# A streamed factorization-machine kernel: the last four input groups as two pairs of 32 KB rows instead of four single ones

## The chip, the core and the metric

The kernel runs on one core of one Trainium2 chip. The metric is the time of one execution in microseconds (us), as the median of several. A core has TensorE (PE in the profile; PEld is its weight load), VectorE (DVE), ScalarE (ACT), GpSimd (POOL) and SyncE (SP), each with its own instruction stream, and 16 DMA engines that move data between the main memory and the on-chip memory SBUF. Engines wait for each other by semaphores.

## The reference

```python
x_reg = input_data @ W_lin.T + b_lin                       # input_data: 1024 x 12500, f32
emb = input_data @ factors                                 # factors: 12500 x 16
sum_squared = jnp.square(emb.sum(axis=1))
squared_sum = (jnp.square(input_data) @ jnp.square(factors)).sum(axis=1)
h = jax.nn.relu(emb @ W1.T + b1)                           # 128
h = jax.nn.relu(h @ W2.T + b2)                             # 64
dnn_out = h @ W3.T + b3
x = x_reg + 0.5 * (sum_squared - squared_sum)[:, None] + dnn_out
x = 0.5 + jax.nn.sigmoid(x) * 5.0
```

The input is 51.2 MB and is read once. All else is small.

## The kernel before

The 12500 dimensions are cut into 97 chunks of 128, one dimension to a partition, and a rest of 84. The 1024 samples are columns. For each chunk TensorE multiplies the chunk of x by 17 weights (16 factors and the linear weight) and the squares of that chunk by 18 (only the last is not zero: minus half the sum of squared factors). Both add into a PSUM bank `p_lin`. VectorE and ScalarE make the squares (`squares`: 3 chunks by VectorE, 3 and 2 by ScalarE). GpSimd copies the weights of a group into small rings `wr` and `wz`.

The input comes in three parts, all issued by SyncE in one queue, in this order:

- 20 **groups** (g = 0 to 19, `TOTAL`) of 8 chunks by 512 samples, 2 MB each. Groups 0 to 11 are the first half of the samples, 12 to 19 two thirds of the second half. They land in six slots of the SBUF buffer `xr`, group g in slot g mod 6.
- The last 32 chunks of the second half, the **end**, in nine **pieces** (`PIECES`, index i): four of 352 samples (12, 10, 6 and 4 chunks; the middle block), then five of 160 samples (8, 8, 8, 6 and 2 chunks; the last block). They land in slots 2 to 5 of `xr` again.

Groups 0 to 15 (`PAIRED` = 16) come two to a transfer of 4 MB, with rows of 32 KB in each partition; groups 16 to 19 come one to a transfer of 2 MB with rows of 16 KB, and each has a semaphore of its own.

The order on TensorE is written out by hand. For a pair (`pair`, line 560) it is: wait for the landing, the matmuls on x of both groups (`multiply` twice), then those on the squares of both (`add_squares` twice). For a single group (lines 661 to 664): wait, `multiply`, `add_squares`. The last matmul of `add_squares` adds one to the semaphore `sq_used`, which starts at `RING` = 3. A slot of `xr` is free when `sq_used` says that its group is done, and SyncE waits for that before each transfer (lines 269, 273, 280):

- pair p waits for group 2p + 1 - 6, so the pair of groups 14 and 15 waits for group 9;
- single group g waits for group g - 6;
- the first two end pieces wait for group 17, the next two for group 18, the other five for group 19.

The end pieces are multiplied by `multiply_end` and `squares_end`, a block's small network (`layer1`, `layer2`, `layer3`, the embedding sums and squares) is woven between them, and SyncE stores each block's result.

Of the kernel before, what the change touches and what calls it, by code (L numbers as in the profile page):

```python
# [14 lines left out]
P = 128  # L15
# [4 lines left out]

REST = N % P
HALF = B // 2
CHUNKS = 8
TWO = 2
SLOTS = 6
RING = 3
ENDS = 32  # L30
ALL = (N - REST) // P
GROUPS = (ALL - 1) // CHUNKS
END_GROUPS = ENDS // CHUNKS
TOTAL = 2 * GROUPS - END_GROUPS
PAIRED = 16
W_END = ALL - ENDS

END_SLOT = TOTAL % SLOTS
# [11 lines left out]

PITCH = CHUNKS * HALF + 64
PAIR_PITCH = TWO * CHUNKS * HALF + 64

# [27 lines left out]
HD = HD_L + REST_SETS * LIN  # L84

def fm_kernel(nc, head, x_first, x_rest, x_pairs, x_groups, x_end, out):
    with ExitStack() as ctx:
        def sb(name, shape, dt=F32):
            return ctx.enter_context(nc.sbuf_tensor(name, shape, dt))  # L90
# [4 lines left out]
        def sem(name):  # L95
            return ctx.enter_context(nc.semaphore(name))
# [4 lines left out]
        xr = sb("xr", [P, SLOTS, CHUNKS, HALF])  # L101
# [33 lines left out]
        first_landed = sem("first_landed")  # L135
        rest_landed = sem("rest_landed")
        x_landed = [sem(f"x_landed{t}") for t in range(SLOTS // TWO)]
        single_landed = [sem(f"single_landed{g}") for g in range(PAIRED, TOTAL)]
        end_landed = [sem(f"end_landed{i}") for i in range(len(PIECES))]
        y_stored = sem("y_stored")  # L140
        zero_set = sem("zero_set")
# [91 lines left out]

            engine.wait_ge(x_landed[s // TWO], 16 * (r + 1))

        def single(engine, g):
            engine.wait_ge(single_landed[g - PAIRED], 16)

        def chunks(i):
            return sum(PIECES[i][2]) + sum(PIECES[i][3])  # L240

# [18 lines left out]
        @block.sync  # L260
        def _(sp):
            sp.dma_start(hd[:, :], head).then_inc(hd_landed, 16)  # L262
            sp.dma_start(xf[:, :], x_first).then_inc(first_landed, 16)  # L263
            sp.dma_start(xl[:, :, :].rearrange("p c b -> p (c b)"), x_rest).then_inc(rest_landed, 16)  # L264
            for p in range(PAIRED // TWO):
                at = TWO * p % SLOTS
                if TWO * p >= SLOTS:

                    sp.wait_ge(sq_used, RING + TWO * p + TWO - SLOTS)
                sp.dma_start(xr[:, at:at + TWO].rearrange("p s c b -> p (s c b)"),  # L270
                             x_pairs[p, :, 0:TWO * CHUNKS * HALF]).then_inc(x_landed[at // TWO], 16)
            for g in range(PAIRED, TOTAL):
                sp.wait_ge(sq_used, RING + g + 1 - SLOTS)
                sp.dma_start(xr[:, g % SLOTS].rearrange("p c b -> p (c b)"),
                             x_groups[g - PAIRED, :, 0:CHUNKS * HALF]).then_inc(single_landed[g - PAIRED], 16)
            at = 0
            for i in range(len(PIECES)):
                c, n = PIECES[i][1], chunks(i)
                rows = x_end[at:at + P * n * width(i)].rearrange("(p m) -> p m", p=P)
                sp.wait_ge(sq_used, RING + TOTAL - SLOTS + END_SLOT + last_slot(i) + 1)  # L280
                sp.dma_start(piece(i, c, n), rows).then_inc(end_landed[i], 16)
                at += P * n * width(i)

            for k in range(len(BLOCKS)):
                sp.wait_ge(y_ready[k], 1)
                sp.dma_start(out[cols(k)].rearrange("(q b) -> q b", q=4), y[0:P:32, line(k)]).then_inc(y_stored, 16)
            sp.wait_ge(y_stored, 16 * len(BLOCKS))
# [26 lines left out]
        @block.scalar  # L314
        def _(act):
            act.wait_ge(zero_set, 1)
            nc.scalar.activation(warm[:, :], zero[:, 0:1], ACT.Sigmoid)
            act.wait_ge(first_landed, 16)
            nc.scalar.activation(sqf[:, :], xf[:, :], ACT.Square).then_inc(first_squared, 1)  # L319

            def squares(r, s):

                act.wait_ge(sq_used, SLOTS * r + s + 1)
                c = BY_DVE
                for n in BY_ACT:
                    nc.scalar.activation(sq[:, ring(s), c:c + n, :], xr[:, s, c:c + n, :],  # L326
                                         ACT.Square).then_inc(act_squared, 1)
                    c += n

            def square_end(i, j=0):  # L330
                c = PIECES[i][1] + sum(PIECES[i][2][:j])
                n = PIECES[i][2][j]
                if j == 0:
                    act.wait_ge(end_landed[i], 16)
                    act.wait_ge(sq_used, squares_free(i))
                nc.scalar.activation(squared_piece(i, c, n), piece(i, c, n),  # L336
                                     ACT.Square).then_inc(act_end_squared, 1)

            def copy_lin(k, u):
                nc.scalar.copy(lin[:, part(k, u)], p_lin[k][:, u * BLOCKS[k][1] // 2:(u + 1) * BLOCKS[k][1] // 2]  # L340
                               ).then_inc(lin_ready[k], 1)

            def layer1(k, n):
                act.wait_ge(p_h1_done[k], 1)
                c = BLOCKS[k][0]
                nc.scalar.activation(h1[:, c:c + n], p_h1[0][:, 0:n], ACT.Relu,
                                     bias=pr[:, C_B1:C_B1 + 1]).then_inc(h1a_ready[k], 1)

            def embedding_square(k):
                act.wait_ge(p_es_done[k], 1)  # L350
                nc.scalar.activation(gsq[:, line(k)], tot_bank(k)[:, line(k)], ACT.Square).then_inc(gsq_ready[k], 1)

            def sigmoid(k):
                act.wait_ge(p_tot_done[k], 1)
                nc.scalar.activation(sg[:, line(k)], tot_bank(k)[:, line(k)], ACT.Sigmoid,
                                     bias=bias[:, :]).then_inc(sg_ready[k], 1)

            with act.Fori(0, GROUPS // SLOTS) as r:
                for s in range(SLOTS):
                    landed(act, r, s)  # L360
                    squares(r, s)

            act.wait_ge(sq_used, RING + GROUPS)
            copy_lin(0, 0)
            copy_lin(0, 1)
            layer1(0, BLOCKS[0][1] // 2)
            embedding_square(0)
            act.wait_ge(bias_ready, 1)
            sigmoid(0)

            for g in range(GROUPS, PAIRED):
                landed(act, g // SLOTS, g % SLOTS)
                squares(g // SLOTS, g % SLOTS)
            for g in range(PAIRED, TOTAL):
                single(act, g)
                squares(g // SLOTS, g % SLOTS)

            square_end(0, 0)
            square_end(0, 1)
            square_end(1, 0)  # L380
            square_end(1, 1)
            square_end(2)
            square_end(3)
            square_end(4, 0)
            act.wait_ge(p_lin_done[1], 1)
            copy_lin(1, 0)
            copy_lin(1, 1)
            nc.scalar.copy(rest[:, :], p_lin[1][:, BLOCKS[1][1]:HALF]).then_inc(rest_copied, 1)
            embedding_square(1)
            square_end(4, 1)  # L390
            layer1(1, BLOCKS[1][1])
            square_end(5, 0)
            square_end(5, 1)
            square_end(6, 0)
            square_end(6, 1)
            square_end(7, 0)
            square_end(7, 1)
            square_end(8)
            sigmoid(1)
            embedding_square(2)  # L400
            act.wait_ge(squares_done, 1)
            nc.scalar.copy(qs[:, :], p_sq[:, 0:BLOCKS[LAST][1]]).then_inc(qs_ready, 1)
            sigmoid(2)

        @block.vector
        def _(dve):
# [16 lines left out]
            def squares(r, s):  # L423

                dve.wait_ge(sq_used, SLOTS * r + s + 1)
                nc.vector.tensor_tensor(sq[:, ring(s), 0:BY_DVE, :], xr[:, s, 0:BY_DVE, :], xr[:, s, 0:BY_DVE, :],  # L426
                                        ALU.mult).then_inc(dve_squared, 1)
# [39 lines left out]
            layer2(0)  # L467
            scale(0)

            for g in range(GROUPS, PAIRED):  # L470
                landed(dve, g // SLOTS, g % SLOTS)
                squares(g // SLOTS, g % SLOTS)
            for g in range(PAIRED, TOTAL):
                single(dve, g)
                squares(g // SLOTS, g % SLOTS)

            square_end(0, 0)
# [24 lines left out]
        def _(pe):  # L502
# [40 lines left out]
            def multiply(r, s, h):  # L543
                pe.wait_ge(wr_ready, SLOTS * r + s + 1)
                for c in range(CHUNKS):
                    add_mm(quad(p_lin[h], c, LIN, 0, HALF), wr[:, ring(s), c, :], xr[:, s, c, :])
# [109 lines left out]
            embedding_square(0)  # L656
            layer3(0)

            for g in range(GROUPS, PAIRED, TWO):
                pair(g // SLOTS, g % SLOTS, 1)  # L660
            for g in range(PAIRED, TOTAL):
                single(pe, g)
                multiply(g // SLOTS, g % SLOTS, 1)
                add_squares(g // SLOTS, g % SLOTS, 1)

            pe.wait_ge(ws_ready, 2)
            for i in range(3):
# [102 lines left out]
```

## Time and profile before

| | us |
|---|---|
| median of 3 runs | 133.88 (133.85 to 133.91) |
| the profiled execution's own time | 133.95 |
| its span in the trace | 132.2 |

| engine | busy us | share of the span |
|---|---|---|
| TensorE, matmuls | 106.2 | 80% |
| TensorE, weight loads | 33.9 | 26% |
| ScalarE | 63.3 | 48% |
| VectorE | 52.5 | 40% |
| GpSimd | 15.5 | 12% |
| SyncE's DMA queue | 52.23 MB | 93.0% of 16 engines |

The span runs from the first to the last instruction in the trace; what lies around it is in the execution's own time. Matmuls are pipelined and their ends are modelled, so a row's time and its successor's start overlap a little: the start of the next row is the better measure of how long work took.

### The profile page before, as it was taken

What the parts mean: (1) busy time and instruction counts of PE and PEld (TensorE: products, weight loads), DVE (VectorE), ACT (ScalarE), POOL (GpSimd) and SP (SyncE); (2) the same over time, 40 slices, a digit from 0 to 9 for tenths busy, and PEclk for the clock granted to TensorE, in tenths of its full rate; (3) what the DMA queues carried; (4) which work ended last, traced back from release to release, by engine and by line L of the source; (5) the groups of instructions that cost most, each with busy time, mean ns of one, the idle gap of its engine ahead of it and who ended that gap; (6) DMA issues with size and microseconds to landing.
All of it is one profiled execution on the core that took longest, in us unless ns stands there. A gap on an engine that the chain in (4) does not pass through costs nothing.

```text
span 132.2 us, 2665 instructions
## 1 busy us (share of the span) xinstructions
PE 106.2 (80%) x1123; PEld 33.9 (26%) x1123; DVE 52.5 (40%) x51; ACT 63.3 (48%) x72; POOL 15.5 (12%) x48
## 2 busy tenths in 40 slices
PE   6089569939839739969649979999997975999992
PEld 4012112112112112212112233222221111335881
DVE  0391063037036036045055016565352351576571
ACT  4030067039139039049059046869562572465851
POOL 3015000110200200110200110064530000000000
PEclk9999968999999977999986999999999999999999
DMA  4999999999999999999999999999999999999700
GB/s 127 409 514 417 426 426 451 426 417 446 417 436 422 446 436 417 426 446 426 426 436 436 426 426 446 392 412 422 436 422 436 417 422 433 408 397 416 284 20 1
DMA packets 3489, 52.36 MB, mean 396 GB/s; under 512 B 404, under 2 KB 536, under 8 KB 1560
## 3 DMA queue, kind: packets, MB, share of 16 engines
q1 hardware_dynamic: 3480, 52.23, 93.0%
q8 instruction: 7, 0.11, 0.4%
q14 instruction: 2, 0.02, 0.0%
HBM read 52.22 MB, written 0.00 MB: 395 GB/s over the span
## 4 chain that ended last, share of the span: by engine, by line
DMA 54%; PE 39%; SPq 2%; DVE 1%; issue 1%; ACT 1%
DMA xr<-in_x_pairs 43%; PE p_lin L504 34%; DMA xr<-in_x_end 11%; PE p_h L600 2%; PE p_sq L504 2%; SPq L270 1%; PE p_tot L504 1%; PE p_h L631 1%; DVE h L452 0%; DVE h L447 0%; PE p_tot L613 0%; SPq L264 0%; SPq L263 0%; SPq L262 0%; ACT lin L340 0%
## 5 line engine op out<-in xcount | busy, mean ns | idle before, releaser
L326 ACT ACTIVATE sq<-xr 128x1536 f32<-128x1536 f32 (+1 forms) x40 | 47.7, 1260 | 45.1 <-DMA xr<-in_x_pairs 37.6
L426 DVE TENSOR_TENSOR sq<-xr 128x1536 f32<-128x1536 f32 x20 | 34.5, 1760 | 53.7 <-DMA xr<-in_x_pairs 42.9
L504 PE MATMUL p_lin<-xr,wr 128*17 128x512 f32 x320 | 41.4, 659 | 16.1 <-DMA xr<-in_x_pairs 14.2
L504 PE MATMUL p_lin<-sq,wz 128*18 128x512 f32 x320 | 36.6, 592 | 0.0
L504 PEld LDWEIGHTS p_lin<-xr,wr 128*17 128x17 f32 x320 | 9.3, 105 | 46.4 <-issue 39.6
L304 POOL COPY wr<-hd 128x136 f32 (+1 forms) x20 | 9.1, 454 | 75.2 <-PE p_lin L504 75.2
L504 PEld LDWEIGHTS p_lin<-sq,wz 128*18 128x18 f32 x320 | 9.5, 98 | 25.0 <-issue 23.7
L504 PE MATMUL p_lin<-xr,hd 128*17 128x352 f32 (+1 forms) x128 | 10.1, 380 | 1.8 <-DMA xr<-in_x_end 1.8
L435 DVE TENSOR_TENSOR sq<-xr 128x1408 f32<-128x1408 f32 (+3 forms) x6 | 6.6, 1133 | 6.2 <-DMA xr<-in_x_end 6.2
L336 ACT ACTIVATE sq<-xr 128x1408 f32<-128x1408 f32 (+3 forms) x6 | 5.7, 981 | 6.3 <-DMA xr<-in_x_end 6.3
L504 PE MATMUL p_lin<-sq,ws 128*18 128x352 f32 x64 | 6.7, 459 | 0.0
L504 PE MATMUL p_lin<-xf,hd 128*17 128x512 f32 x4 | 3.6, 1049 | 3.5 <-DMA xf<-in_x_first 3.5
L504 PEld LDWEIGHTS p_lin<-xr,hd 128*17 128x17 f32 x128 | 4.3, 97 | 5.9 <-issue 4.1
L305 POOL COPY wz<-s_all 128x8 f32 (+1 forms) x20 | 5.4, 271 | 0.0
L435 DVE TENSOR_TENSOR xr<-xr 128x320 f32<-128x320 f32 (+1 forms) x9 | 3.8, 450 | 2.1 <-DMA xr<-in_x_end 2.1
L504 PE MATMUL p_sq<-xr,ws 128*18 128x160 f32 x64 | 4.1, 300 | 0.0
L336 ACT ACTIVATE xr<-xr 128x320 f32<-128x320 f32 (+1 forms) x9 | 3.4, 431 | 0.9 <-DMA xr<-in_x_end 0.8
L447 DVE TENSOR_SCALAR h<-p_h,hd 128x256 f32<-128x256 f32 (+1 forms) x2 | 0.9, 433 | 7.2 <-PE p_h L600 7.2
L409 DVE SCALAR_TENSOR_TENSOR fsq<-hd 128x1552 f32<-128x1552 f32 x1 | 1.8, 1777 | 4.4 <-DMA hd<-in_head 4.4
L319 ACT ACTIVATE sqf<-xf 128x1024 f32<-128x1024 f32 x1 | 1.1, 1057 | 4.6 <-DMA xf<-in_x_first 4.6
L340 ACT COPY lin<-p_lin 128x256 f32<-128x256 f32 (+1 forms) x4 | 1.2, 342 | 4.1 <-PE p_lin L504 4.1
L504 PEld LDWEIGHTS p_lin<-sq,ws 128*18 128x18 f32 x64 | 2.4, 97 | 2.4 <-issue 1.7
(52 smaller groups left out, 39.7 us busy)
## 6 DMA issues: line engine op xcount, KB each, us to landing
xr<-in_x_pairs SPq DMA_DIRECT2D x8, 4096.0 KB, 22.0
xr<-in_x_groups SPq DMA_DIRECT2D x4, 2048.0 KB, 18.2
xr<-in_x_end SPq DMA_DIRECT2D x1, 2112.0 KB, 10.6
xr<-in_x_end SPq DMA_DIRECT2D x3, 640.0 KB, 12.6
xr<-in_x_end SPq DMA_DIRECT2D x1, 1760.0 KB, 14.5
xr<-in_x_end SPq DMA_DIRECT2D x1, 1056.0 KB, 13.0
hd<-in_head SPq DMA_DIRECT2D x1, 952.0 KB, 4.8
xr<-in_x_end SPq DMA_DIRECT2D x1, 704.0 KB, 14.3
```

The source lines that it names most:

```text
L270: sp.dma_start(xr[:, at:at + TWO].rearrange("p s c b -> p (s c b)"), x_pairs[p, :, 0:TWO * CHUNKS * HALF]).then_inc(x_landed[at // TWO], 16)
L304: nc.gpsimd.tensor_copy(wr[:, ring(s), :, :], w[:, bass.ds(at, CHUNKS), :]).then_inc(wr_ready, 1)
L305: nc.gpsimd.tensor_copy(wz[:, ring(s), :, LIN:WZ].rearrange("p c k -> p (c k)"), s_all[:, bass.ds(at, CHUNKS)]).then_inc(wz_ready, 1)
L326: nc.scalar.activation(sq[:, ring(s), c:c + n, :], xr[:, s, c:c + n, :], ACT.Square).then_inc(act_squared, 1)
L336: nc.scalar.activation(squared_piece(i, c, n), piece(i, c, n), ACT.Square).then_inc(act_end_squared, 1)
L340: nc.scalar.copy(lin[:, part(k, u)], p_lin[k][:, u * BLOCKS[k][1] // 2:(u + 1) * BLOCKS[k][1] // 2]).then_inc(lin_ready[k], 1)
L409: nc.vector.scalar_tensor_tensor(fsq[:, :, :], w[:, :, 0:EMB], -0.5, w[:, :, 0:EMB], ALU.mult, ALU.mult).then_inc(fsq_ready, 1)
L426: nc.vector.tensor_tensor(sq[:, ring(s), 0:BY_DVE, :], xr[:, s, 0:BY_DVE, :], xr[:, s, 0:BY_DVE, :], ALU.mult).then_inc(dve_squared, 1)
L435: nc.vector.tensor_tensor(squared_piece(i, c, n), piece(i, c, n), piece(i, c, n), ALU.mult).then_inc(dve_end_squared, 1)
L504: return nc.tensor.matmul(out, lhsT, rhs, start=False, stop=False, skip_group_check=True)
L600: mm = nc.tensor.matmul(bank[32 * t:32 * t + 32, 0:n], pr[:, C_W1 + 32 * t:C_W1 + 32 * t + 32], rhs, start=True, stop=True, skip_group_che ...
L631: mm = nc.tensor.matmul(p_h2[32 * t:32 * t + 32, row(k)], pr[:, C_W2 + t % 2 * 32:C_W2 + t % 2 * 32 + 32], h1[:, part(k, t // 2)], start=T ...
```

## The change

All 20 groups are stored and loaded in pairs. The loop over single groups goes from SyncE, VectorE, ScalarE and TensorE, with its four semaphores. Groups 16 and 17 (slots 4 and 5) and groups 18 and 19 (slots 0 and 1) share one landing each, on the semaphores `x_landed` that the earlier pairs use. By the rule for pairs, 16 and 17 wait for group 11 and 18 and 19 for group 13. The end pieces are untouched.

```diff
-            for p in range(PAIRED // TWO):
+            for p in range(TOTAL // TWO):
                 at = TWO * p % SLOTS
                 if TWO * p >= SLOTS:
 
                     sp.wait_ge(sq_used, RING + TWO * p + TWO - SLOTS)
                 sp.dma_start(xr[:, at:at + TWO].rearrange("p s c b -> p (s c b)"),
                              x_pairs[p, :, 0:TWO * CHUNKS * HALF]).then_inc(x_landed[at // TWO], 16)
-            for g in range(PAIRED, TOTAL):
-                sp.wait_ge(sq_used, RING + g + 1 - SLOTS)
-                sp.dma_start(xr[:, g % SLOTS].rearrange("p c b -> p (c b)"),
-                             x_groups[g - PAIRED, :, 0:CHUNKS * HALF]).then_inc(single_landed[g - PAIRED], 16)
...
-            for g in range(GROUPS, PAIRED):
+            for g in range(GROUPS, TOTAL):
                 landed(act, g // SLOTS, g % SLOTS)
-                squares(g // SLOTS, g % SLOTS)
-            for g in range(PAIRED, TOTAL):
-                single(act, g)
                 squares(g // SLOTS, g % SLOTS)
...
-            for g in range(GROUPS, PAIRED, TWO):
+            for g in range(GROUPS, TOTAL, TWO):
                 pair(g // SLOTS, g % SLOTS, 1)
-            for g in range(PAIRED, TOTAL):
-                single(pe, g)
-                multiply(g // SLOTS, g % SLOTS, 1)
-                add_squares(g // SLOTS, g % SLOTS, 1)
```

VectorE has the same edit as ScalarE, and the host lays the input out to match.

The order on TensorE at groups 16 and 17, before. `xr,wr` are matmuls on x, `sq,wz` on squares; what a matmul waits for stands in brackets.

```order
L504 MATMUL p_lin<-xr,wr 17x512 [waits wr_ready,single_landed16]
L504 MATMUL p_lin<-xr,wr 17x512 x7
L504 MATMUL p_lin<-sq,wz 18x512 [waits act_squared,dve_squared,wz_ready]
L504 MATMUL p_lin<-sq,wz 18x512 x5
L504 MATMUL p_lin<-sq,wz 18x512 [waits act_squared]
L504 MATMUL p_lin<-sq,wz 18x512
L504 MATMUL p_lin<-xr,wr 17x512 [waits wr_ready,single_landed17]
L504 MATMUL p_lin<-xr,wr 17x512 x7
```

The same place after the change:

```order
L487 MATMUL p_lin<-xr,wr 17x512 [waits wr_ready,x_landed2]
L487 MATMUL p_lin<-xr,wr 17x512 x7
L487 MATMUL p_lin<-xr,wr 17x512 [waits wr_ready]
L487 MATMUL p_lin<-xr,wr 17x512 x7
L487 MATMUL p_lin<-sq,wz 18x512 [waits act_squared,dve_squared,wz_ready]
L487 MATMUL p_lin<-sq,wz 18x512 x5
L487 MATMUL p_lin<-sq,wz 18x512 [waits act_squared]
```

The matmuls on x of group 17 moved ahead of the squares of group 16, and group 16's wait is now for the landing of both. On SyncE, the transfers before, from the fourth pair to the second end piece:

```order
L270 DMA xr<-in_x_pairs 128x8192 [waits sq_used] x5
L274 DMA xr<-in_x_groups 128x4096 [waits sq_used] x4
L281 DMA xr<-in_x_end 128x4224 [waits sq_used]
L281 DMA xr<-in_x_end 128x3520 [waits sq_used]
```

And after:

```order
L263 DMA xr<-in_x_pairs 128x8192 [waits sq_used] x7
L270 DMA xr<-in_x_end 128x4224 [waits sq_used]
L270 DMA xr<-in_x_end 128x3520 [waits sq_used]
```

Two transfers took the place of four; nothing passed anything else in the queue.

## Rows read from the trace of the kernel before

**Rows 1.** The page: DMA share and granted TensorE clock in 40 slices, tenths.

```profile
PEclk9999968999999977999986999999999999999999
DMA  4999999999999999999999999999999999999700
```

**Rows 2.** The chain of waits: start us, us, what.

```profile
0.74 0.39 SPq L262
...
38.45 7.10 PE p_lin L504 x64
...
45.57 22.04 DMA xr<-in_x_pairs
...
101.08 0.33 SPq L281
...
115.96 6.76 PE p_lin L504 x92
```

**Rows 3.** Timeline of TensorE, groups: start us, us, line, output<-inputs, count, [idle before].

```profile
17.63 5.15 PE L504 MATMUL p_lin<-xr,wr 128*17 128x512 f32 x32 [2.45 <-DMA xr<-in_x_pairs]
...
28.73 3.63 PE L504 MATMUL p_lin<-xr,wr 128*17 128x512 f32 x32 [2.52 <-DMA xr<-in_x_pairs]
...
38.45 3.63 PE L504 MATMUL p_lin<-xr,wr 128*17 128x512 f32 x32 [2.66 <-DMA xr<-in_x_pairs]
...
48.29 5.18 PE L504 MATMUL p_lin<-xr,wr 128*17 128x512 f32 x32 [2.77 <-DMA xr<-in_x_pairs]
...
58.01 3.63 PE L504 MATMUL p_lin<-xr,wr 128*17 128x512 f32 x32 [1.11 <-DMA xr<-in_x_pairs]
...
67.73 5.32 PE L504 MATMUL p_lin<-xr,wr 128*17 128x512 f32 x32 [2.66 <-DMA xr<-in_x_pairs]
...
87.09 3.63 PE L504 MATMUL p_lin<-xr,wr 128*17 128x512 f32 x32
90.54 3.62 PE L504 MATMUL p_lin<-sq,wz 128*18 128x512 f32 x32
93.97 1.90 PE L504 MATMUL p_lin<-xr,wr 128*17 128x512 f32 x16
...
101.76 1.91 PE L504 MATMUL p_lin<-xr,wr 128*17 128x512 f32 x16 [0.74 <-DMA xr<-in_x_groups]
...
106.67 1.91 PE L504 MATMUL p_lin<-xr,wr 128*17 128x512 f32 x16 [1.15 <-DMA xr<-in_x_groups]
```

**Rows 4.** Timeline of VectorE, which starts on a group when it lands.

```profile
28.73 3.43 DVE L426 TENSOR_TENSOR sq<-xr 128x1536 f32<-128x1536 f32 x2 [7.67 <-DMA xr<-in_x_pairs]
...
87.07 3.53 DVE L426 TENSOR_TENSOR sq<-xr 128x1536 f32<-128x1536 f32 x2 [2.60 <-DMA xr<-in_x_pairs]
...
106.65 1.76 DVE L426 TENSOR_TENSOR sq<-xr 128x1536 f32<-128x1536 f32 x1 [3.15 <-DMA xr<-in_x_groups]
```

**Rows 5.** Stretches: busy us per engine, then granted clock, DMA share, GB/s.

```profile
1.75:2.00 0.25, 0.25 (x3) 0.15 (x1) 0.00 (x0) 0.25 (x1) 0.02 (x1) 1.00 1.48 244
...
48.00:50.00 2.00, 1.71 (x12) 0.37 (x16) 1.71 (x2) 1.73 (x2) 0.00 (x0) 0.51 0.99 426
...
58.00:60.00 2.00, 1.99 (x20) 0.62 (x24) 2.00 (x2) 2.00 (x2) 0.00 (x0) 1.00 0.91 393
...
126.00:128.00 2.00, 2.00 (x65) 1.64 (x60) 1.61 (x6) 1.32 (x5) 0.00 (x0) 1.00 0.05 11
```

**Rows 6.** Timeline of TensorE, end pieces: first, second, first of the last block.

```profile
111.80 1.97 PE L504 MATMUL p_lin<-xr,hd 128*17 128x352 f32 x24 [1.38 <-DMA xr<-in_x_end]
...
115.96 1.66 PE L504 MATMUL p_lin<-xr,hd 128*17 128x352 f32 x18 [0.41 <-DMA xr<-in_x_end]
...
121.90 0.82 PE L504 MATMUL p_lin<-xr,hd 128*17 128x160 f32 x14
```

**Rows 7.** Timeline of ScalarE where the middle block's sums are copied.

```profile
121.88 0.47 ACT L336 ACTIVATE xr<-xr 128x320 f32<-128x320 f32 x1 [0.79 <-DMA xr<-in_x_end]
122.36 0.51 ACT L340 COPY lin<-p_lin 128x176 f32<-128x176 f32 x2
```

More of the change, by code:

```diff
@@ L34 @@
 TOTAL = 2 * GROUPS - END_GROUPS
-PAIRED = 16
 W_END = ALL - ENDS
@@ L49 @@
 BY_ACT = (3, 2)
-PITCH = CHUNKS * HALF + 64
 PAIR_PITCH = TWO * CHUNKS * HALF + 64
@@ L84, with fm_kernel @@
 HD = HD_L + REST_SETS * LIN
-def fm_kernel(nc, head, x_first, x_rest, x_pairs, x_groups, x_end, out):
+def fm_kernel(nc, head, x_first, x_rest, x_pairs, x_end, out):
     with ExitStack() as ctx:
@@ L137, in fm_kernel @@
         x_landed = [sem(f"x_landed{t}") for t in range(SLOTS // TWO)]
-        single_landed = [sem(f"single_landed{g}") for g in range(PAIRED, TOTAL)]
         end_landed = [sem(f"end_landed{i}") for i in range(len(PIECES))]
@@ L234, in landed @@
             engine.wait_ge(x_landed[s // TWO], 16 * (r + 1))
-        def single(engine, g):
-            engine.wait_ge(single_landed[g - PAIRED], 16)
         def chunks(i):
@@ L468, in _ @@
             scale(0)
-            for g in range(GROUPS, PAIRED):
+            for g in range(GROUPS, TOTAL):
                 landed(dve, g // SLOTS, g % SLOTS)
-                squares(g // SLOTS, g % SLOTS)
-            for g in range(PAIRED, TOTAL):
-                single(dve, g)
                 squares(g // SLOTS, g % SLOTS)
@@ L657, in _ @@
             layer3(0)
-            for g in range(GROUPS, PAIRED, TWO):
+            for g in range(GROUPS, TOTAL, TWO):
                 pair(g // SLOTS, g % SLOTS, 1)
-            for g in range(PAIRED, TOTAL):
-                single(pe, g)
-                multiply(g // SLOTS, g % SLOTS, 1)
-                add_squares(g // SLOTS, g % SLOTS, 1)
             pe.wait_ge(ws_ready, 2)
@@ L728 @@
     chunks = xT[P + REST:].reshape(ALL - 1, P, B)
-    x_pairs = np.zeros((PAIRED // TWO, P, PAIR_PITCH), f32)
-    x_groups = np.zeros((TOTAL - PAIRED, P, PITCH), f32)
+    x_pairs = np.zeros((TOTAL // TWO, P, PAIR_PITCH), f32)
     for g in range(TOTAL):
         h, c = g // GROUPS, CHUNKS * (g % GROUPS)
-        rows = chunks[c:c + CHUNKS, :, h * HALF:(h + 1) * HALF].transpose(1, 0, 2).reshape(P, -1)
-        if g < PAIRED:
-            at = g % TWO * CHUNKS * HALF
-            x_pairs[g // TWO, :, at:at + CHUNKS * HALF] = rows
-        else:
-            x_groups[g - PAIRED, :, :CHUNKS * HALF] = rows
+        at = g % TWO * CHUNKS * HALF
+        x_pairs[g // TWO, :, at:at + CHUNKS * HALF] = chunks[c:c + CHUNKS, :, h * HALF:(h + 1) * HALF].transpose(1, 0, 2).reshape(P, -1)
     ends = chunks[ALL - 1 - ENDS:]
@@ L761 @@
     params[:, C_B3] = np.asarray(L0_rec_b3)
-    arrays = {"head": head, "x_first": x_first, "x_rest": x_rest, "x_pairs": x_pairs, "x_groups": x_groups, "x_end": x_end}
+    arrays = {"head": head, "x_first": x_first, "x_rest": x_rest, "x_pairs": x_pairs, "x_end": x_end}
     nc = bacc.Bacc("TRN2", target_bir_lowering=False, num_devices=1)
```

## The prediction, made before the changed kernel ran

> **What bounds the kernel now.** I read the page first, for the DMA row and the clock row [rows 1]. The DMA engines are full in every slice but the first and the last three, so for some 120 us the kernel runs at the pace of its input stream. The clock row has dips in the first half and none in the last.
>
> Then the chain of waits [rows 2]. It ends in a stretch of TensorE work that starts at 115.96 us, when the second end piece has landed, and it does not come back to a transfer before the last instruction. So the end is set by TensorE from 115.96 on. The stream has 10 us to go at that point (in 126 to 128 us the DMA share is 0.05 [rows 5]), and the two run nearly level: 92 matmuls in 6.76 us are 73.5 ns each, and the four pieces of the middle block are worked off about as they land. Any lag that TensorE has at 115.96 is therefore a candidate for the end.
>
> Next TensorE in order of time [rows 3], for how much it has to spare while pairs arrive. A pair of groups takes 87.09 to 93.97, which is 6.88 us, and pairs land every 9.7 us. The reader is to see the idle time in brackets: 2.5 to 2.8 us before most pairs, but 0.74 us before group 18 and 1.15 us before group 19, which came alone. Last the landings, as the moments at which VectorE starts [rows 4].
>
> **What leaves and what takes its place.** Four transfers of 2 MB (groups 16 to 19) become two of 4 MB. Nothing is computed differently; no instruction of VectorE, ScalarE or GpSimd is added or removed. TensorE has the same matmuls in another order: all 32 matmuls on x of two groups, then their 32 on squares, and one wait on a landing where there were two.
>
> Step 1, the stream. Pairs 1 to 7 land between 28.73 and 87.07 us, six steps, so 58.34 / 6 = 9.72 us a pair [rows 4]. The singles take 106.65 - 87.07 = 19.58 us for four. Two pairs would take 19.45 us. The last pair lands at 106.51 instead of 106.65, and all that follows in the stream comes 0.14 us earlier. The bounds are 0 (the single rows were no slower by themselves) and 0.3.
>
> A page of the Trainium skill, DMA: Bandwidth & Descriptors, section Anatomy of one DMA, gives a transfer issued by another path a fixed cost of about 2.0 us beside its bytes, and its rules for kernel authors ask to coalesce. Taken as time of the stream, two transfers fewer would give back an estimated 4.0 us and the sum would be 4 us lower. The landings say otherwise: singles come every 4.89 us and half a pair is 4.86 us, so the fixed part already lies under the transfers queued ahead.
>
> Step 2, the issue. The transfer of groups 16 and 17 waits for group 11 and that of 18 and 19 for group 13. Two pairs, some 19 us of stream, are queued ahead each time, so this costs nothing. The edge is the first end piece, which waits for group 17. Before, group 17 was finished and the piece issued at 101.08 [rows 2]. Now group 17 arrives with 16 at 87.07 + 9.72 = 96.79 and the pair has to be worked off. One pair landing at 38.45 let go the next transfer 7.10 us later [rows 2], so the piece is issued at 103.9, with the queue holding data until 106.5. That leaves 2.6 us. At the start of the kernel the first issue began at 0.74 [rows 2] and the first bytes moved by 2.0 us [rows 5], 1.3 us at most. The margin covers it; I take 0. The third and fourth piece wait for group 18, the rest for group 19, done near 111.7 (three quarters of the last pair's work) and 113.4, while the first two keep the queue full to about 115.9: again 0.
>
> Step 3, TensorE on the last four groups, which is the term that decides. Before, groups 16 and 17 were begun without a pause after group 15, and at 106.67 only group 19 was left: done about 3.45 us later, with 1.38 us of idle time before the first end piece [rows 3, 6]. Now the pair 16 and 17 starts at 96.8 and ends at 103.7, then TensorE idles. The pair 18 and 19 starts at 106.53 and takes 6.88 us: it ends at 113.41, when the first end piece has been there for almost 2 us. That piece has 12 chunks, 48 matmuls at 73.5 ns, 3.53 us. The second piece is thus begun at 116.94 instead of 115.96 [rows 6]: **a lag of 0.98 us**. The idle time that hid the work of one group is used up, and the rest is lag.
>
> Step 4, what the tail gives back. From 115.96 to the first piece of the last block at 121.90 TensorE is busy without a break, so nothing is given back there. After that it meets short waits on ScalarE. The copies of the sums start at 122.36, right behind a square that began at 121.88 and took 0.47 us [rows 7]. With TensorE later, this square is out of the way, which gives back up to 0.2 us; the waits for the last landings disappear as well, up to about 0.1. The remaining waits are for copies and layers that follow TensorE and shift with it. I take 0.2 us; the bounds are 0 and 0.5, since the chain shows TensorE without a real gap.
>
> **Sum.** 0.98 - 0.2 = +0.8 us on the span: 132.2 to 133.0, and the profiled execution's own 133.95 to 134.75 (what lies around the span is 1.75 us and does not change). The profiled execution is 0.07 above the median of 133.88, so the median becomes **134.7 us**. With the bounds of steps 1 and 4 it is 134.2 to 135.0.
>
> **Rivals.**
>
> *The last pair meets the low clock.* The pairs that landed at 17.63, 48.29 and 67.73 took 5.15 to 5.32 us for their first 32 matmuls where the others took 3.63 [rows 3]; the granted clock was 0.51 in 48 to 50 us and 1.00 in 58 to 60 [rows 5], that is the 1.2 GHz level instead of 2.4. All three came after 2.45 to 2.77 us of idle time. Of five pairs with such a pause three were slow; the one after 1.11 us of pause was not. In the stream of before these slow starts cost nothing, for 2.7 us of waiting followed. The singles had pauses of 1.15 us at most and the clock stayed up. The change makes two new pauses of about 2.7 us, before each of the last pairs. A slow start of 16 and 17 is harmless: the pair ends at 105.4, the next pause shrinks to 1.1 us, and the first end piece is issued at 105.5, which leaves 1 us. A slow start of 18 and 19 goes straight to the lag: 5.15 to 5.32 minus 3.63 is about 1.6 us, hence 136.3 us. It needs a normal 16 and 17 (about a half) and a slow 18 and 19 (again a half), a quarter at most; I give it 0.2.
>
> *The lag is swallowed, no loss.* If the matmuls of the end only look continuous and could run closer together when all data is there, the end would still follow the last landing, between 126 and 127 us, and move with the stream by -0.14: 133.7 us, no change. That decides if TensorE can give back 0.98 us between 117 and 128.7 us. For it: busy matmuls are modelled. Against it: 73.5 ns a matmul is the same for work that had been waiting and for work that had just landed. 0.1.
>
> *The queue runs dry before the end pieces.* It takes over if an issue at 103.9 moves no data until after 106.5. A delay of 1 us beyond that makes the second piece land at 116.9, just when TensorE wants it, and the pieces of the last block land up to 1 us late: about 134.9. 0.05; it lies in the range.
>
> *Larger transfers are worth a fixed cost each.* At 2.0 us for each of two transfers saved it would be about 130. The landings speak against it, as said; so does a stream that already moves 4 MB every 9.7 us. 0.03.
>
> **How the numbers follow.** A change of 0.2%, 0.27 us, is about what a measurement of this kernel can tell from none. Forecast 0.62, low clock 0.2 and dry queue 0.05 are slower: 0.87. The swallowed lag, 0.1, is no change in 0.09 and, with a stream gain at its bound of 0.3, faster in 0.01; with the fixed cost, 0.03, faster has 0.04. The range has to reach the low clock, since forecast and dry queue hold only 0.67: 134.2 to 136.5, leaving out the swallowed lag and the fixed cost. The forecast's own range is 134.2 to 135.0.
>
> **What would show it.** VectorE's start on groups 18 and 19 at 106.5 with no pause between them, and the last landings 0.1 to 0.2 us earlier than before: step 1. First end piece issued at about 103.9 and the DMA row still full around 106: step 2. TensorE idle for 2.7 us before 96.8 and before 106.5, no idle time before the first end piece, the second begun near 116.9: step 3. The last output about 0.8 us later: step 4. A granted clock below 1 after 96 us, with the first 32 matmuls of a pair taking over 5 us, means the low clock. I am wrong if TensorE is idle before the second end piece, or if the pieces of the last block are taken up at their old times.

## The result: 2% slower, and not by one fixed amount

The changed kernel takes 136.56 us as the median of four executions (137.42, 137.07, 135.19, 136.05) against 133.89 for the kernel before. A second set of six gave 136.83 (135.0 to 137.48). The ratio with its interval is 1.0169 [1.0145, 1.0192]; it leaves out executions over 1.5% above the kernel's fastest, which here belong to the kernel's own spread, so the medians say more. The kernel before spreads over 0.1 us in the same executions. The prediction was 134.7 us with a range of 134.2 to 136.5: the sign was right, the loss 2.7 us instead of 0.8, and the median just outside the range.

The profiled execution took 137.42 us, its span 135.6. The page of the changed kernel, clock and DMA share in 40 slices of 3.4 us, to set beside [rows 1]:

```profile
PEclk9999977977999977999999999999779999999999
DMA  4999999999999998999989999999996699999500
```

Both rows have something new: the clock falls in the 29th and 30th slice (95 to 102 us), and the DMA share in the 31st and 32nd (102 to 108 us). A stream that never paused before now does. TensorE in order of time (start us, us, line, output<-inputs, count, [idle before]), the rows that answer to [rows 3] and [rows 6]:

```profile
90.42 3.62 PE L487 MATMUL p_lin<-sq,wz 128*18 128x512 f32 x32
96.69 5.32 PE L487 MATMUL p_lin<-xr,wr 128*17 128x512 f32 x32 [2.65 <-DMA xr<-in_x_pairs]
101.83 3.62 PE L487 MATMUL p_lin<-sq,wz 128*18 128x512 f32 x32
106.41 3.63 PE L487 MATMUL p_lin<-xr,wr 128*17 128x512 f32 x32 [0.97 <-DMA xr<-in_x_pairs]
109.86 3.62 PE L487 MATMUL p_lin<-sq,wz 128*18 128x512 f32 x32
113.48 1.97 PE L487 MATMUL p_lin<-xr,hd 128*17 128x352 f32 x24
...
117.67 1.66 PE L487 MATMUL p_lin<-xr,hd 128*17 128x352 f32 x18 [0.44 <-DMA xr<-in_x_end]
```

The pair of groups 16 and 17 started at the low clock: 5.32 us for its first 32 matmuls instead of 3.63. The stretch of 97 to 100 us, with the granted clock third from the end, shows 0.50:

```profile
97.00:100.00 3.00, 3.00 (x18) 0.58 (x14) 3.00 (x2) 3.00 (x3) 0.00 (x0) 0.50 0.96 415
```

The pair of 18 and 19 was normal, and the first end piece followed it without a pause at 113.48, as step 3 had it. But TensorE then waited 0.44 us for the second piece, which the prediction had named as the sign that it is wrong. SyncE's issues in the same trace:

```profile
85.50 0.33 SPq L263 DMA_DIRECT2D xr<-in_x_pairs  x1
105.51 10.30 SPq L270 DMA_DIRECT2D xr<-in_x_end  x9
```

and the landings, by VectorE's starts (last pair, first, second and third end piece, first of the last block):

```profile
106.39 3.43 DVE L412 TENSOR_TENSOR sq<-xr 128x1536 f32<-128x1536 f32 x2 [6.30 <-DMA xr<-in_x_pairs]
113.37 2.43 DVE L421 TENSOR_TENSOR sq<-xr 128x1408 f32<-128x1408 f32 x2 [3.55 <-DMA xr<-in_x_end]
117.65 2.06 DVE L421 TENSOR_TENSOR sq<-xr 128x1408 f32<-128x1408 f32 x2 [1.85 <-DMA xr<-in_x_end]
121.50 1.26 DVE L421 TENSOR_TENSOR sq<-xr 128x1056 f32<-128x1056 f32 x1 [1.79 <-DMA xr<-in_x_end]
...
124.82 0.90 DVE L421 TENSOR_TENSOR xr<-xr 128x320 f32<-128x320 f32 x2 [0.69 <-DMA xr<-in_x_end]
```

The last pair landed 0.26 us earlier than group 19 did before [rows 4]. In the kernel before, the second piece was begun at 115.96 and the last block at 121.90 [rows 6]; here they come 1.7 and 2.9 us later, and each time because the data is late. The chain of waits agrees: it now goes back through a transfer of the end pieces until 121.48, where it left them at 115.9 before.

```profile
106.41 5.39 PE p_lin L487 x48
...
111.82 9.66 DMA xr<-in_x_end
...
121.52 4.14 PE p_lin L487 x52
```

The hole itself, in stretches of 1 us (busy us of each engine, then granted clock, DMA share, GB/s):

```profile
103.00:104.00 1.00, 1.00 (x16) 0.26 (x12) 0.00 (x0) 0.00 (x0) 0.18 (x1) 1.00 0.56 229
104.00:105.00 1.00, 1.00 (x16) 0.21 (x8) 0.00 (x0) 0.00 (x0) 0.26 (x2) 1.00 0.31 131
105.00:106.00 1.00, 0.44 (x6) 0.00 (x0) 0.00 (x0) 0.00 (x0) 0.00 (x0) 1.00 0.00 0
106.00:107.00 1.00, 0.59 (x8) 0.25 (x12) 0.61 (x1) 0.61 (x1) 0.00 (x0) 1.00 1.01 220
107.00:108.00 1.00, 1.00 (x16) 0.23 (x8) 1.00 (x1) 1.00 (x2) 0.00 (x0) 1.00 0.62 203
```

```profile
103.50:104.50 1.00, 1.00 (x16) 0.33 (x12) 0.00 (x0) 0.00 (x0) 0.44 (x2) 1.00 0.01 0
104.50:104.75 0.25, 0.25 (x8) 0.02 (x4) 0.00 (x0) 0.00 (x0) 0.00 (x0) 1.00 1.22 524
104.75:106.00 1.25, 0.69 (x8) 0.00 (x0) 0.00 (x0) 0.00 (x0) 0.00 (x0) 1.00 0.00 0
106.25:106.50 0.25, 0.09 (x4) 0.09 (x8) 0.11 (x1) 0.11 (x1) 0.00 (x0) 1.00 1.11 270
```

```profile
DMA packets 12, 0.00 MB, mean 0 GB/s; under 512 B 12, under 2 KB 12, under 8 KB 12
```

The other four come between 105.83 and 105.96, and VectorE starts on the pair at 106.39. The landing, which is the last event of a transfer, says that the queue still had work when the first end piece was issued at 105.51. In fact twelve of the 16 engines had been idle for 1.0 to 1.6 us by then. The first packets of the piece begin at 106.46, 0.95 us after the issue, and the flow is back at its full rate only at about 108.3. The Trainium skill says the same of the semaphore: in DMA: Bandwidth & Descriptors, section Why a DMA increments its semaphore by 16 and not by 1, up to 16 engines finish independently and only the full count means that all data has landed.

### The profile page after: what moved, and what is told of

It reads as the page before. It is cut to its first block, busy times and chain, and to the rows that moved or that the text cites. A ratio compares the mean times of both kernels' runs of the same rounds, so it can differ in the third digit from the quotient of the medians.

```text
span 135.6 us, 2661 instructions
## 1 busy us (share of the span) xinstructions
PE 109.8 (81%) x1123; PEld 34.7 (26%) x1123; DVE 52.3 (39%) x51; ACT 63.1 (47%) x72; POOL 10.8 (8%) x48
## 4 chain that ended last, share of the span: by engine, by line
DMA 64%; PE 29%; SPq 2%; issue 1%; DVE 1%; ACT 1%
DMA xr<-in_x_pairs 57%; PE p_lin L487 24%; DMA xr<-in_x_end 7%; PE p_sq L487 2%; PE p_h L583 2%; PE p_tot L487 1%; SPq L263 1%; PE p_h L614 1%; DVE h L438 0%; DVE h L433 0%; SPq L257 0%; SPq L256 0%; SPq L255 0%; ACT lin L329 0%; PE p_tot L603 0%
## 5 line engine op out<-in xcount | busy, mean ns | idle before, releaser
L487 PE MATMUL p_lin<-xr,wr 128*17 128x512 f32 x320 | 42.9, 684 | 16.9 <-DMA xr<-in_x_pairs 16.9
L293 POOL COPY wr<-hd 128x136 f32 (+1 forms) x20 | 5.9, 297 | 85.3 <-PE p_lin L487 85.3
L294 POOL COPY wz<-s_all 128x8 f32 (+1 forms) x20 | 3.9, 197 | 0.0
L583 PE MATMUL p_h<-lin,hd 128*32 128x256 f32 (+2 forms) x32 | 2.5, 382 | 0.5 <-ACT lin L329 0.5
```

The costliest lines, as they stand in the source:

```text
L293: nc.gpsimd.tensor_copy(wr[:, ring(s), :, :], w[:, bass.ds(at, CHUNKS), :]).then_inc(wr_ready, 1)
L294: nc.gpsimd.tensor_copy(wz[:, ring(s), :, LIN:WZ].rearrange("p c k -> p (c k)"), s_all[:, bass.ds(at, CHUNKS)]).then_inc(wz_ready, 1)
L487: return nc.tensor.matmul(out, lhsT, rhs, start=False, stop=False, skip_group_check=True)
L583: mm = nc.tensor.matmul(bank[32 * t:32 * t + 32, 0:n], pr[:, C_W1 + 32 * t:C_W1 + 32 * t + 32], rhs, start=True, stop=True, skip_group_che ...
```

## The experiments

Two theories stood after the result. **Theory Q**: the queue runs dry before the end pieces, because the pair of groups 16 and 17 is done late, more so when it starts at the low clock. **Theory L**: the prediction's own terms, TensorE's lag and a slow start of the last pair, make up the whole loss.

**More executions of the changed kernel**, with no edit.

> The changed kernel unaltered, for more executions of it. Both theories: between 135.2 and 137.4 us, spread by where the low-clock stretches fall. Theory Q (the queue runs dry): the DMA share has a hole of 1 to 3 us near 104 to 107 us in this trace too, and the first end piece lands after 112.0. Theory L (TensorE's lag plus low clock on the last pair): the trace shows the last pair slow in a slow execution.

Measured: 137.04, 136.63, 136.32, 135.0, 137.48 and 137.19 us. The trace of the first (137.04) shows the same picture as above: 16 and 17 slow (5.32 us), the first end piece issued at 105.56 and landed at 113.36, the DMA share 0.00 in 105 to 106 us. Its second piece came later still: TensorE begins it at 119.09, after 1.88 us of idle time. This profile again has the slow start on 16 and 17 and not on the last pair, against what theory L expected.

**Early issue of the end pieces.** The rule for the end pieces waits two groups longer than their slots of `xr` need. The edit removes that, and nothing else:

```diff
-                sp.wait_ge(sq_used, RING + TOTAL - SLOTS + END_SLOT + last_slot(i) + 1)
+                sp.wait_ge(sq_used, RING + TOTAL - SLOTS + last_slot(i) + 1)
```

> The changed kernel with each end piece waiting only for the group that really frees its slots, two groups earlier (the first piece for group 15 instead of 17), so that it is issued near 94 us. Theory Q: no hole in the stream, the first end piece lands at 111.5, and what is left is the lag of TensorE: about 134.7 us (134.2 to 135.0), 136.3 only where the last pair starts at the low clock. Theory L: the queue never mattered, so the time stays at 136.6 (135.2 to 137.4).

Measured: 134.76, 134.76, 134.79, 134.85, 136.26 and 136.34 us, median 134.82. The first end piece is issued at 94.07. The stretches of the hole in this trace:

```profile
104.00:105.00 1.00, 0.00 (x0) 0.00 (x0) 0.00 (x0) 0.00 (x0) 0.00 (x0) 1.00 1.13 470
105.00:106.00 1.00, 0.00 (x0) 0.00 (x0) 0.00 (x0) 0.00 (x0) 0.00 (x0) 1.00 1.02 422
106.00:107.00 1.00, 0.51 (x8) 0.20 (x12) 0.53 (x1) 0.53 (x1) 0.00 (x0) 1.00 0.87 372
107.00:108.00 1.00, 1.00 (x16) 0.28 (x12) 1.00 (x1) 1.00 (x2) 0.00 (x0) 1.00 1.11 473
```

Over 104 to 108 us they sum to 1737 GB/s against 554 in the changed kernel: 1183 GB/s for 1 us, at the 426 GB/s of a full stream 2.8 us of transfer. By the packets of the changed kernel's trace, spread over the time that they took, some 1.9 us of it are lost before 106.5, while engines are idle, and 0.9 us after it, while the stream starts again. TensorE in this trace:

```profile
96.66 3.63 PE L487 MATMUL p_lin<-xr,wr 128*17 128x512 f32 x32 [2.65 <-DMA xr<-in_x_pairs]
...
106.49 3.63 PE L487 MATMUL p_lin<-xr,wr 128*17 128x512 f32 x32 [2.77 <-DMA xr<-in_x_pairs]
...
113.37 1.96 PE L487 MATMUL p_lin<-xr,hd 128*17 128x352 f32 x24
115.14 1.96 PE L487 MATMUL p_lin<-sq,ws 128*18 128x352 f32 x24
116.92 1.65 PE L487 MATMUL p_lin<-xr,hd 128*17 128x352 f32 x18
```

This is step 3 of the prediction within 0.02 us: the second piece begun at 116.92, predicted 116.94, and a time of 134.8, predicted 134.7. The two executions at 136.3 stand where the prediction put a slow last pair; neither was traced, so that they are such executions is not shown here. The prediction's sum was right for a kernel whose queue never runs dry. Theory L falls as the whole story; its terms stay.

**Each pair alone.** With 18 and 19 as a pair and 16 and 17 single:

```diff
-            for g in range(PAIRED, TOTAL):
+            for g in range(PAIRED, PAIRED + 2):
                 single(pe, g)
                 multiply(g // SLOTS, g % SLOTS, 1)
                 add_squares(g // SLOTS, g % SLOTS, 1)
+            pair(TOTAL // SLOTS, 0, 1)
```

> Only groups 18 and 19 as a pair, 16 and 17 single as before. The first end piece is issued near 101.1 as before. Theory Q: no hole, lag alone: about 134.7 us, up to 136.3 with a slow last pair. Theory L: the last pair does all the harm, so as much as the whole change, 136.6 us.

Measured: 136.93 us (136.71 to 137.63). The expectation of theory Q was missed. I had not counted the pause: TensorE is through with 17 before the pair arrives and idles 5.61 us, not 2.7.

```profile
98.94 1.90 PE L513 MATMUL p_lin<-sq,wz 128*18 128x512 f32 x16
106.45 5.21 PE L513 MATMUL p_lin<-xr,wr 128*17 128x512 f32 x32 [5.61 <-DMA xr<-in_x_pairs]
```

The pair starts slow in the trace, and all five executions are long. It is also late enough to hold back the third piece, which waits for group 18: that group is done near 113.3 us here (the squares of both begin at 111.49) and near 111.7 in the changed kernel. Here the share falls later, behind the first two pieces:

```profile
113.00:114.00 1.00, 1.00 (x12) 0.21 (x8) 0.48 (x1) 0.49 (x1) 0.00 (x0) 1.00 0.43 171
114.00:115.00 1.00, 1.00 (x16) 0.29 (x12) 1.00 (x1) 1.00 (x2) 0.00 (x0) 1.00 0.76 180
115.00:116.00 1.00, 1.00 (x20) 0.34 (x16) 1.00 (x3) 0.90 (x2) 0.00 (x0) 1.00 0.72 279
```

So this run joins three effects (lag, low clock, late third piece) and separates nothing; it was done again below without two of them.

With 16 and 17 as a pair and 18 and 19 single (`PAIRED` = 18):

> Only groups 16 and 17 as a pair, 18 and 19 single as before. The first end piece is issued at 103.9, or at 105.5 when the pair starts slow. Theory Q: the hole is there without any lag of TensorE: the last landings come 0.5 to 2 us late, 134.4 to 136.0 us. Theory L: TensorE has no lag at the second end piece, so 133.8 us, no change against the kernel before.

Measured: 134.72, 134.88, 135.15, 135.41, 136.26 and 136.48 us. Theory L's 133.8 is excluded. In the trace (136.48) the pair started slow, the first end piece was issued at 105.45 and landed at 113.25; TensorE idled 1.12 us before it, so it had no lag there and still came out 2.6 us over the kernel before. The slow start that the prediction called harmless costs an estimated 1.6 us through the queue. This is the distance from the two lowest times to the two highest, of which only 136.48 was traced.

**Keeping the clock up.** Zero matmuls (`FILL` = 10) in the pauses before both pairs, in the changed kernel with and without early issue:

```diff
             for g in range(GROUPS, TOTAL, TWO):
+                if g >= TOTAL - 4:
+                    for _ in range(FILL):
+                        nc.tensor.matmul(p_h1[1][:, :], zero[:, 0:P], zero[:, :], start=True, stop=False,
+                                         skip_group_check=True)
                 pair(g // SLOTS, g % SLOTS, 1)
```

> The changed kernel with early issue of the end pieces and, before each of the last two pairs, ten matmuls of 512 columns of zeros into a bank that nothing reads, so that TensorE works through most of the 2.7 us pause. Theory now: loss = hole in the stream + lag 0.9 us + 1.6 us when the last pair starts at the low clock. With hole and low clock gone only the lag stays: 134.8 us in every execution, none near 136.3. Rival, that the upper cluster of 136.3 comes from something else than the clock: a third of the executions stay there.

Measured: 134.57 to 134.77 us in five executions, median 134.7. The cluster at 136.3 is gone. Five executions alone would not say much, since four of six had stayed below it without the zeros; the six of the last experiment, with the last pair and zeros before it, have none either. In the trace the zeros leave 0.28 us of pause before 16 and 17, 0.39 us before 18 and 19, and both pairs run at full clock:

```profile
94.38 2.10 PE L646 MATMUL p_h<-zero 128*128 128x512 bf16 x9 [0.16 <-issue]
96.77 3.63 PE L488 MATMUL p_lin<-xr,wr 128*17 128x512 f32 x32 [0.28 <-DMA xr<-in_x_pairs]
```

> The changed kernel with the ten zero matmuls before each of the last two pairs, end pieces issued by the old rule (first piece at 103.9). Theory now: no slow pair, so the hole shrinks to what an issue at 103.9 leaves, and lag stays: 135.0 us in every execution, like the fastest of the changed kernel. Rival, that the low clock is not what makes the long executions long: spread 135.0 to 137.5 as before.

Measured: 134.78, 134.84, 135.0, 135.07, 135.14 and one at 136.17 us, median 135.04. As expected, but for the one, of which there is no trace. In the profiled execution the first end piece was issued at 103.74 and the second landed on time (115.74), but the third at 119.32 instead of 118.56 in the kernel before. An issue 2.6 us ahead of the last landing already leaves a hole: its first packets begin at 104.70, again 0.95 us after the issue, and twelve engines had reported between 103.66 and 104.47. In the stretch of 103 to 107 us this trace moves 1038 GB/s for 1 us and the early issue 1510, a difference of 1.1 us of transfer, of which 0.8 show at the third piece. It mattered little, since TensorE was late anyway.

**Early issue in the kernel before.**

> The kernel before with the early issue of the end pieces. Theory now: its stream has no hole, so nothing to gain: 133.9 us. Rival, that the old rule costs the kernel before something too: 133.5 or less.

Measured: 133.85 us (133.73 to 134.0, eleven executions), ratio 0.9999 [0.9991, 1.0008]. The old rule costs the kernel before nothing.

**Single transfers, pair order.** Four transfers of 2 MB as before, but both landings awaited and the matmuls in the order of a pair:

```diff
-            for g in range(PAIRED, TOTAL):
+            for g in range(PAIRED, TOTAL, TWO):
                 single(pe, g)
+                single(pe, g + 1)
                 multiply(g // SLOTS, g % SLOTS, 1)
+                multiply(g // SLOTS, g % SLOTS + 1, 1)
                 add_squares(g // SLOTS, g % SLOTS, 1)
+                add_squares(g // SLOTS, g % SLOTS + 1, 1)
```

> Groups 16 to 19 still come in four transfers of 2 MB, but every engine waits for both of two and TensorE takes them in the order of a pair. Theory now: the landing of two at once does the harm, not the size of the rows, so the same as the changed kernel, 135.0 to 137.5 with two clusters. Rival, that the 4 MB transfers with rows of 32 KB let the DMA engines drift apart and so cause the hole: 134.8 to 136.3, as with the early issue.

Measured: 136.8 us (136.5 to 138.05). The rows of 32 KB do not make the hole: with 16 KB rows it is there too (DMA share 0.15 in 105 to 106 us, first piece issued at 105.63 and landed at 113.60). The trace has the slow start on 16 and 17 again (5.32 us). Five of the six executions lie between 136.5 and 137.0 and one at 138.05; the lower cluster near 135 did not show. Why none was as short as 135 stays open.

**The hole alone.** The kernel before, with singles, no lag and full clock, but each end piece held back by one group more:

```diff
-                sp.wait_ge(sq_used, RING + TOTAL - SLOTS + END_SLOT + last_slot(i) + 1)
+                sp.wait_ge(sq_used, min(RING + TOTAL, RING + TOTAL - SLOTS + END_SLOT + last_slot(i) + 2))
```

> The kernel before, with singles and without any lag or low clock at the end, but each end piece waits for one group more: the first is issued when group 18 is done, near 105.4 us, which is still 1.2 us before group 19 lands. Theory E (most DMA engines run dry well before the landing that the last of them signals): a hole like the changed kernel's, the first end piece lands 1.5 to 2 us late, the end 1.5 to 2.5 us later, 135.4 to 136.4 us. Rival (the queue holds work until the landing, as the prediction took it): no hole, 133.9 us.

Measured: 137.13 us (136.43 to 138.0): more than the upper end of what was expected. Its issues and landings:

```profile
105.52 8.21 SPq L281 DMA_DIRECT2D xr<-in_x_end  x9
```

```profile
106.57 1.76 DVE L426 TENSOR_TENSOR sq<-xr 128x1536 f32<-128x1536 f32 x1 [3.12 <-DMA xr<-in_x_groups]
113.86 2.43 DVE L435 TENSOR_TENSOR sq<-xr 128x1408 f32<-128x1408 f32 x2 [5.53 <-DMA xr<-in_x_end]
118.06 2.06 DVE L435 TENSOR_TENSOR sq<-xr 128x1408 f32<-128x1408 f32 x2 [1.77 <-DMA xr<-in_x_end]
121.33 1.26 DVE L435 TENSOR_TENSOR sq<-xr 128x1056 f32<-128x1056 f32 x1 [1.21 <-DMA xr<-in_x_end]
```

An issue at 105.52, 1.05 us ahead of the last landing, costs 2.2 us at the first piece (TensorE begins it at 113.97 instead of 111.80 [rows 6]) and 2.8 at the third (118.56 in the kernel before). A queue that held work until the landing would have shown neither. No order on TensorE and no transfer differs from the kernel before; the late issue alone does this. It does open a pause of 3.63 us before the first end piece. The clock stayed up in the traced execution (136.74), but the longest one (138.0) has a mean granted clock of 0.925, against 0.960 to 0.975 in the other five. The low clock may thus be part of the time beyond what was expected; no trace shows it.

**Each pair alone, again, with the queue fed and the clock up.**

> Groups 16 and 17 as a pair, 18 and 19 single, end pieces issued early, ten zero matmuls before the pair. Theory now: neither hole nor lag is left, so this pair alone costs nothing: 133.8 to 133.9 us, and the 0.07 us of the stream is all that it could gain. Rival, that a pair on TensorE costs something by itself: 134.3 or more.

Measured: 134.03 us (133.91 to 134.32, eleven executions), ratio 1.0013 [1.0004, 1.0021]: 0.1 us above what was expected, below the 134.3 of the rival. The pair of 16 and 17 by itself costs next to nothing.

> Groups 16 and 17 single, 18 and 19 as a pair, end pieces issued early, 24 zero matmuls (some 5.1 us) in the pause of 5.6 us before the pair. Theory now: all of the lag is in this pair, 134.7 us in every execution, as with both pairs. Rival, that the lag needs both pairs: 133.9 us.

Measured: 134.93 us (134.68 to 135.09), 0.2 us above what was expected and far from the 133.9 of the rival. All of the lag is in the last pair.

| kernel | us, median | what is in it |
|---|---|---|
| before | 133.89 | |
| pair 16/17 alone, early, zeros | 134.03 | |
| pair 18/19 alone, early, zeros | 134.93 | lag |
| both pairs, early, zeros | 134.70 | lag |
| both pairs, early | 134.82, two of six at 136.3 | lag, low clock at times |
| both pairs, zeros | 135.04 | lag, small hole |
| both pairs (the change) | 136.56 and 136.83 | lag, hole, low clock |
| singles, end pieces late | 137.13 | hole |

No version beat the kernel before. What the change could win, a stream faster by 0.03 us for each 2 MB, cannot reach an end that TensorE sets. The table also splits the loss of the change: 0.9 us are the lag (134.82), and the other 1.7 to 2.0 us go with the late issue. Most of these need the slow start of 16 and 17 too, for with the clock kept up the late issue costs 0.3 us (135.04 against 134.70).

## Why the prediction was wrong

- **Step 1, the stream**, held: the last pair landed at 106.39 (predicted 106.51).
- **Step 2, the issue**, is the step that failed. It put the late issue at nothing, because it took the queue to hold data until the landing at 106.5: an issue at 103.9 had 2.6 us to spare and one at 105.5 still 1 us. Measured, as lateness of the third end piece against the kernel before: 5.6 us ahead of the landing loses nothing (the kernel before, as its early issue shows), 2.6 us ahead loses 0.8 and 1.05 us ahead loses 2.8. The landing is that of the slowest of 16 engines. Twelve had reported 1.9 to 2.5 us before it, the last four 0.4 to 0.6 us before it, and the first packets come 0.95 us after an issue. For twelve engines the last moment to issue without a gap was thus between 102.9 and 103.5, an estimate (103.89 and 104.47 less 0.95), where step 2 had 105.2 (106.5 less 1.3). The trace of before could have told: group 19 landed at 106.65, and of its 16 reports twelve lie between 103.77 and 104.63 and four between 106.03 and 106.15. The shares per stretch hide it there, since the next transfer follows at once. That the third piece has time until group 18 is done was right for the changed kernel, and wrong where the last pair was slow (pair 18/19 alone).
- **Step 3, the lag**, held where it can be seen alone: 116.92 for 116.94.
- **Step 4, the tail**, held: +0.8 us with both pairs, the queue fed and the clock up (134.70).
- **The rival of the low clock** fits in mechanism (the slow last pair traced with pair 18/19 alone took 5.21 us) and in size (136.3 in the early version, untraced, predicted 136.3), but was wrong in its line that a slow start of 16 and 17 is harmless. In both profiles of the changed kernel that was the slow one, and it was in four of the five traces in which these two groups were worked off together with no zeros before them, where the prediction gave it a half. It moved the issue from 103.7 (the version with zeros) to 105.5, onto the steep part of step 2. So the low clock had two places to do harm, and one of them was given no price.
- **The rival of the dry queue** named the right place and was priced at 0.2 us over the forecast, with a chance of 0.05. It measured 2.8 us of stream and 1.7 to 2.0 us of the median time. It was mis-sized because it let every engine start again 1 us late at most, measured from the landing.
- The swallowed lag and the fixed cost of a transfer did not show.
- One reading was inexact: the third dip of the clock in [rows 1] lies just behind the middle, at 66 to 73 us. Nothing rested on it.

## What to carry to other kernels

The margin of a DMA queue ends well before the landing of its last transfer: ask how many us before that landing the next one is issued, and take only a margin that was seen to hold (here 5.6 us did and 2.6 us did not). Read a landing as the end of the slowest engine, and a share of 0.00 as a stretch in which no packet began. Grouping two units of work saves next to nothing once the fixed part lies under queued transfers, but it delays what the first unit frees and leaves two units to work off after the last landing. Where a group's end frees a slot, a slow clock on it is paid by the stream, even if its own engine has time.

## What the runs showed of the hardware

- The 16 DMA engines are spread widely at a transfer's end. In the trace of the change twelve reported the last pair 1.9 to 2.5 us before VectorE started on it and four 0.4 to 0.6 us before. In the kernel before, with the queue full and rows of 16 KB, it was 2.0 to 2.9 us and 0.5 to 0.6 us.
- From an issue on SyncE to its first packet with all or most engines idle it took 0.95 us (105.51 to 106.46 in the change, 103.74 to 104.70 with the zeros, 105.52 to 106.47 with the late issue in the kernel before).
- After the hole the stream came back slowly: the first packets of 16.9 KB took up to 1.6 us, later ones 0.63. This restart makes 0.9 of the 2.8 us lost.
- A pause of TensorE of 2.65 us brought the clock down to 1.2 GHz in one trace (the change, 96.69 us) and not in another (early issue, 96.66 us). In all 13 traces together the starts of pairs divide like this: after 1.91 us of pause or less, none of 41 was slow; after 1.98 to 2.94 us, 27 of 50; after 3.82 us or more, all nine. The one pause of 3.63 us, before the first end piece with the late issue, left the clock up. That the same kernel has times of 135.0 and 137.5 fits this, but no execution of it near 135.0 was traced.
- Zero matmuls in the pause, 2.1 of 2.7 us, kept the clock at 2.4 GHz in both traced versions and took the spread from 1.6 to 0.2 us where the queue was fed.
